# A three-part decoder layer on one core: the first feed-forward group's routing laid between the pieces of the last cross-attention step

## The chip, the cores and the metric

The kernel runs on one core of a Trainium2 chip. The metric is the device time of one execution in microseconds. The median of three runs before the change is 622.98 us (621.36 to 623.25). The engines are TensorE (PE, with its weight loads as PEld), VectorE (DVE), ScalarE (ACT), GpSimd (POOL) and SyncE (SP). Each runs its own queue strictly in the order written, and they meet at semaphores.

## What is computed

The input is a stream x of 32 batches of 128 x 128 floats. Three blocks follow each other, each a layer norm, a block and a residual addition.

```python
x = x + gated_slot_attention(layernorm(x))                    # recurrent, 4 heads
x = x + cross_attention(layernorm(x), ctx, bias, mask)        # 16 heads of 8, full softmax
x = x + experts(layernorm(x))
# experts: logits = h @ gate_w.T + gate_b; scores = softmax(logits); top-2 of 8
# for e in range(8):
#   gate  = (times e is among the two) * (sum of the two scores)
#   inter = h @ wi.T + bi + (h @ lora_A[e].T) @ lora_B[e].T
#   out  += gate * (relu(inter) @ wo.T + bo)
```

## The kernel before

The kernel has three stages, one per block. Each is a software pipeline: a step function per engine (x_tensor, x_scalar, x_vector and x_pool for cross attention; f_tensor, f_scalar, f_vector and f_pool for the feed-forward) holds that engine's share of one step, with flags that say which phases a step has. Steady steps stand in a loop; the first and the last are written out ("peeled") by x_peeled and f_peeled, which work out the flags. The order of the work is the order of these calls in each engine's block, written out by hand; there is no planner.

**Cross attention.** A step n handles one batch in each phase: it normalises batch n+3, projects batch n+2, makes the scores of batch n+1, turns the attention weights of batch n ("attend"), and finishes batch n-1. Step 30 has scores of batch 31, attends to batch 30 and finishes batch 29. Step 31 attends to batch 31 and finishes batch 30, and has no scores left. Step 32 only finishes batch 31. In a step ScalarE takes 16 exponentials of 128 x 128 in four groups of four (L960), TensorE transposes each group (L916), VectorE or ScalarE copies it out of PSUM (L1056 on VectorE, L986 on ScalarE), TensorE mixes the values (L927), VectorE multiplies by the reciprocals (L1051), TensorE applies the output weight (L903), and VectorE adds the result to the stream X (L1070). VectorE also makes the reciprocals (L1060) and spreads them (L1065); TensorE turns these (L888) and ScalarE copies them (L981).

**Feed-forward.** A tick f(t) handles groups of four batches: it normalises group t+1, routes group t and runs the experts of group t-1. Tick f(-1) only normalises group 0, and tick f(0) normalises group 1 and routes group 0 without expert work. f(1) is the first full tick, f(1) to f(6) have the same load, and f(7) is the last that routes and normalises nothing. The route on the engines:

- TensorE: x_turned (L1210, four transposes), logits (L1217), lora_inner (L1223), choices_turned (L1230, eight transposes).
- ScalarE: the copy of the transposes (L1298), gate_exps (L1316), the lora copies (L1308, L1311), x_high (L1303).
- VectorE: statistics (L1351, L1355), logits (L1368 to L1371), ranks (L1376 to L1386), choices (L1394, L1395), gates (L1399 to L1407), chosen_inner (L1415), normalise (L1362).
- POOL: x_low (L1471), roots (L1464, L1467), u_low (L1475), output_bias (L1481, L1484).

The expert work on TensorE is L1236 and L1260, with L1293 on ScalarE and L1422 and L1431 on VectorE.

**Where the two stages meet.** Every engine's block ends its cross stage in the same order: the tick f(-1), then steps 30 and 31, then f(0), then step 32, then f(1) and the loop. TensorE waits before f(0) until all scores have been taken out of their PSUM banks (the tick writes the same banks), and before f(1) until every batch has its cross output:

```python
x_peeled(cross, 30); x_peeled(cross, 31)
pe.wait_ge(C["tt"], 4 * B)
f_peeled(experts, 0)
x_peeled(cross, B)
pe.wait_ge(C["x2"], B)
f_peeled(experts, 1)
```

(B is 32; the first line is a loop in the source.)

Of the kernel before, what the change touches and what calls it, by code (L numbers as in the profile page):

```python
# [15 lines left out]
B, T, D = 32, 128, 128  # L16
# [8 lines left out]
GROUPS = B // GROUP  # L25
# [25 lines left out]
def decoder(nc, x, ctx_in, fside, amask, kmask, g_wq, g_wk, g_wv, g_wf, g_norm, g_wo,  # L51
# [6 lines left out]
    with stack:  # L58
# [801 lines left out]

        SCORE_BANKS = (1, 4, 5, 6)

        def x_tensor(pe, m, q, norm, project, scores, attend, finish):
            n = 2 * m + q
            o = 1 - q

            def all_scores():

                need(pe, C["q"], n + 2)
                need(pe, C["kbd"], n + 2)  # L870
                need(pe, C["tt"], 4 * n + 4)
                for i in range(NI):
                    rows = slice(32 * i, 32 * i + 32)
                    nc.tensor.matmul(bank(SCORE_BANKS[i]), qx[rows, o, :], kbd[rows, o, :, :].rearrange("p j s -> p (j s)"),  # L874
                                     start=True, stop=True).then_inc(C["sc"], 1)

            def inputs_turned():
                need(pe, C["xn"], n + 3)
                need(pe, s_ctx[q], 16 * (m + 2))
                need(pe, C["x2"], n - 1)  # L880
                need(pe, C["v"], n + 1)
                nc.tensor.transpose(bank(0)[:, 0:128], xn2[:], ident[:])
                nc.tensor.transpose(bank(0)[:, 128:256], ctxb[:, q, :], ident[:]).then_inc(C["Tp"], 1)
# [45 lines left out]
                                                PTs[:, o, i, 128 * j:128 * j + 128], start=(j == 0), stop=(j == XG - 1))  # L929
                last.then_inc(C["pv"], 1)  # L930

            if scores:
                all_scores()
            if project:
                inputs_turned()
            if finish:
                reciprocals_turned()
            if attend:
                weights_turned(0)
                weights_turned(1)  # L940
            if project:
                queries_keys()
            if finish:
                mix_values()
            if attend:
                weights_turned(2)
            if scores or finish:
                outputs_values()
            if attend:
                weights_turned(3)  # L950

        def x_scalar(act, m, q, norm, project, scores, attend, finish):
            n = 2 * m + q
            o = 1 - q

            def exps(batch, par, i):

                need(act, C["tt"], 4 * batch + i + 1)
                for h in range(XG * i, XG * i + XG):
                    last = nc.scalar.activation(P[:, par, h, :], P[:, par, h, :], ACT.Exp, bias=mn[:, par, h:h + 1], scale=-1.0,  # L960
                                                accum_out=rsx[:, par, h:h + 1])
                last.then_inc(C["ex"], 1)

            def inputs_turned():
# [12 lines left out]

            def reciprocals_turned():
                need(act, C["Rp"], n)
                need(act, C["oT"], n - 1)  # L980
                nc.scalar.copy(RT[:], bank(7)[:, 0:128]).then_inc(C["RT"], 1)  # L981

            def weights_turned():
                need(act, C["pt"], 4 * n + 4)
                need(act, C["pv"], n - 1)
                nc.scalar.copy(PTs[:, q, 3, :], bank(3)).then_inc(C["ptA"], 1)  # L986

            if attend:
                exps(n, q, 1)
            if project:  # L990
                inputs_turned()
            if finish:
                reciprocals_turned()
            if attend:
                exps(n, q, 2)
            if project:
                queries_keys()
            if attend:
                exps(n, q, 3)
            if scores:  # L1000
                exps(n + 1, o, 0)
            if attend:
                weights_turned()

        def x_row(m, q, k):

            n = 2 * m + q + k
            return X[:, n, :] if isinstance(n, int) else X[:, bass.ds(n, 1), :].rearrange("p a d -> p (a d)")

        def x_vector(dve, m, q, norm, project, scores, attend, finish):  # L1010
            n = 2 * m + q
            o = 1 - q

# [64 lines left out]
            if project:  # L1078
                masks()
            if norm:  # L1080
                statistics()
                aggregates()
            if scores:
                score(0)
            if attend:
                weights_turned(0)
            if scores:
                score(1)
            if attend:
                weights_turned(1)  # L1090
            if scores:
                score(2)
            if finish:
                outputs()
            if scores:
                score(3)
            if attend:
                weights_turned(2)
            if scores:
                values()  # L1100
            if finish:
                add_to_stream()
            if attend:
                reciprocals()
                reciprocals_spread()
            if norm:
                normalise()

        def x_pool(pool, m, q, norm, project, scores, attend, finish):
            n = 2 * m + q  # L1110

            def output_bias():
# [28 lines left out]
                roots()  # L1141

        def x_peeled(step, n):
            step(n // 2, n % 2, *(0 <= n + k < B for k in (3, 2, 1, 0, -1)))

        def x_loop(engine, step):
            with engine.Fori(1, B // 2 - 2, 1) as m:
# [52 lines left out]
        s_out = [sem(f"stored{i}") for i in range(2)]  # L1201

        def f_tensor(pe, m, q, norm, route, expert):
            t = 2 * m + q
            def x_turned():
                need(pe, M["xn"], t + 1)
# [53 lines left out]
                                                woT[:, c, :], start=(c == 0), stop=(c == FC - 1))  # L1261
                last.then_inc(M["y"], 1)

            if route:
                x_turned()
            if expert:
                first(0)
            if route:
                logits()
            if expert:  # L1270
                second(0)
                first(1)
            if route:
                lora_inner()
            if expert:
                second(1)
# [1 line left out]
                first(3)  # L1278
                second(2)
                second(3)  # L1280
            if route:
                choices_turned()
            if expert:
                down()

        def f_scalar(act, m, q, norm, route, expert):
            t = 2 * m + q
            p = t - 1

# [28 lines left out]
            if route:  # L1318
                x_turned()
            if expert:  # L1320
                relu(0)
            if route:
                gate_exps()
            if expert:
                relu(1)
            if route:
# [6 lines left out]
        def f_vector(dve, m, q, norm, route, expert):  # L1333
            t = 2 * m + q
            p, o = t - 1, 1 - q

# [98 lines left out]
            if norm:  # L1435
                statistics()
            if route:
                logits()
            if expert:
                hidden(0)  # L1440
            if route:
                ranks()
            if expert:
                hidden(1)
            if route:
                choices()
                gates()
            if expert:
                hidden(2)
                hidden(3)  # L1450
            if route:
                chosen_inner()
            if norm:
                normalise()
            if expert:
                add_to_stream()

        def f_pool(pool, m, q, norm, route, expert):
            t = 2 * m + q

            def roots():
# [24 lines left out]
            if route:  # L1486
                x_low()
            if norm:
                roots()
            if route:  # L1490
                u_low()
                output_bias()

        def f_peeled(tick, t):
            tick(t // 2, t % 2, *(0 <= t + k < GROUPS for k in (1, 0, -1)))

        def f_loop(engine, tick):
            with engine.Fori(1, GROUPS // 2 - 1, 1) as m:
# [26 lines left out]
        def _(pool):  # L1526
# [28 lines left out]
                x_peeled(cross, n)  # L1555
            pool.wait_ge(C["xn"], B)
            f_peeled(experts, -1)
            for n in range(B - 2, B):
                x_peeled(cross, n)
            f_peeled(experts, 0)  # L1560
            x_peeled(cross, B)
            f_peeled(experts, 1)
            f_loop(pool, experts)
# [4 lines left out]
        def _(act):  # L1568
# [27 lines left out]
            act.wait_ge(s_small, SMALL)  # L1596
            act.wait_ge(G["x1"], PAIRS)
            f_peeled(experts, -1)
            for n in range(B - 2, B):
                x_peeled(cross, n)  # L1600
            f_peeled(experts, 0)
            x_peeled(cross, B)
            f_peeled(experts, 1)
            f_loop(act, experts)
# [4 lines left out]
        def _(dve):  # L1609
# [43 lines left out]
            for n in range(B - 2, B):  # L1653
                x_peeled(cross, n)
            f_peeled(experts, 0)
            x_peeled(cross, B)
            dve.wait_ge(C["x2"], B)
            f_peeled(experts, 1)
# [5 lines left out]
        def _(pe):  # L1664
# [37 lines left out]
            for n in range(B - 2, B):  # L1702
                x_peeled(cross, n)
            pe.wait_ge(C["tt"], 4 * B)
            f_peeled(experts, 0)
            x_peeled(cross, B)
            pe.wait_ge(C["x2"], B)
            f_peeled(experts, 1)
# [27 lines left out]
```

## Time and profile before

| | |
|---|---|
| median of three runs | 622.98 us (621.36 to 623.25) |
| the profiled execution's own time | 620.23 us |
| its span, from first to last instruction | 618.5 us |
| mean granted TensorE clock | 0.96 |
| busy: TensorE / VectorE / ScalarE / POOL | 511.4 / 497.3 / 432.0 / 369.5 us |

The rows are from one execution. Times count from the start of the span. "Idle before" in brackets is the time for which the engine had nothing to run ahead of the row, and names what ended it.
### The profile page before, as it was taken

Reading aid. Unit: us, or ns where it says so; the run is one execution under the profiler, and the core shown is the slowest. Engines: PE = TensorE matmul, PEld = TensorE weight load, DVE = VectorE, ACT = ScalarE, POOL = GpSimd, SP = SyncE. Lnnn points to the kernel's source line nnn. Section 1 sums busy time; section 2 is a strip of 40 time slices with the busy share of each in tenths; the row PEclk is TensorE's granted clock in tenths of the full one; section 3 lists DMA queues with packets and bytes.
Section 4 is the critical chain, followed back from the end, with each engine's and each line's share of the span. In section 5 each row is a group of like instructions: output and inputs, shape, how many; then the busy total and the mean of one; then the engine's idle time right before and its main releaser. Section 6 shows DMA issues by size and latency. Waiting matters only on the chain. (4 is left out here: it accounts for less than half of the span.)

```text
span 618.5 us, 15993 instructions
## 1 busy us (share of the span) xinstructions
PE 511.4 (83%) x4272; PEld 380.2 (61%) x4272; DVE 497.3 (80%) x2009; ACT 432.0 (70%) x1545; POOL 369.5 (60%) x392
## 2 busy tenths in 40 slices
PE   4689999999996768777777777777766899999986
PEld 3466777777774445555555555555545678788874
DVE  2677888888876269999999999999986788898872
ACT  2668787887872269999999999999984333333321
POOL 6236554555534778888888888888932233444430
PEclk9899999999998669999999999999997799999999
DMA  6910000000000447888888888888700000000000
GB/s 159 239 21 1 1 2 0 0 0 0 2 1 2 72 98 130 144 144 146 144 145 143 149 146 145 147 147 147 119 2 2 0 18 19 17 17 17 19 18 17
DMA packets 84422, 42.37 MB, mean 69 GB/s; under 512 B 4378, under 2 KB 84132, under 8 KB 84388
## 3 DMA queue, kind: packets, MB, share of 16 engines
q1 hardware_dynamic: 83234, 41.63, 36.6%
q10 hardware_dynamic: 1154, 0.33, 0.2%
q8 instruction: 16, 0.26, 0.2%
q14 instruction: 18, 0.15, 0.1%
HBM read 39.86 MB, written 2.10 MB: 68 GB/s over the span
## 5 line engine op out<-in xcount | busy, mean ns | idle before, releaser
L960 ACT ACTIVATE c_P<-c_P,c_min 128x128 f32<-128x128 f32 x512 | 204.7, 461 | 0.0
L1129 POOL TENSOR_TENSOR c_bias<-c_fside,c_cm 128x2048 f32<-128x2048 f32 x32 | 145.4, 4545 | 2.7 <-DVE c_cm L1046 2.7
L960 ACT ACTIVATION_READ_ACCUMULATOR c_P<-c_P,c_min 128x1 f32 x512 | 132.8, 260 | 0.0
L1021 DVE CUSTOM_DVE_ANT_0 c_P<-banks,c_bias 128x128 f32<-128x128 f32 x512 | 117.0, 285 | 7.9 <-issue 3.6
L916 PE MATMUL banks<-ident,c_P 128*128 128x128 f32 x512 | 80.7, 286 | 8.1 <-ACT c_P L960 6.4
L916 PEld LDWEIGHTS banks<-ident,c_P 128*128 128x128 f32 x512 | 57.5, 144 | 22.6 <-ACT c_P L960 12.9
L1056 DVE COPY shared<-banks 128x512 f32<-128x512 f32 x96 | 65.9, 686 | 2.8 <-PE banks L916 2.8
L1471 POOL TENSOR_TENSOR xs<-shared,xs 128x512 fp32r<-128x512 f32 x8 | 10.7, 1343 | 85.7 <-ACT xs L1303 85.7
L1236 PE MATMUL banks<-um,lb_s 128*128 128x512 f32 x192 | 55.7, 405 | 2.7 <-ACT shared L1293 1.9
L1293 ACT ACTIVATE shared<-banks,bi_col 128x512 f32<-128x512 f32 x32 | 22.0, 688 | 38.9 <-PE banks L1236 38.9
L903 PE MATMUL banks<-x_wT,shared 128*128 128x128 f32 x64 | 15.2, 321 | 40.1 <-DVE shared L1051 40.1
L1236 PEld LDWEIGHTS banks<-um,lb_s 128*128 128x128 f32 x192 | 34.4, 189 | 18.9 <-ACT shared L1293 12.4
L793 POOL TENSOR_TENSOR shared<-shared 128x512 f32<-128x512 f32 x16 | 20.4, 1275 | 38.4 <-ACT shared L584 38.4
L1021 DVE DVE_READ_ACCUMULATOR2_ANT c_min<- 128x1 f32 x512 | 42.5, 83 | 0.0
L874 PE MATMUL banks<-shared,c_q 32*128 32x512 f32 x256 | 38.4, 670 | 2.4 <-DVE X L726 0.5
L903 PEld LDWEIGHTS banks<-x_wT,shared 128*128 128x128 f32 x64 | 10.0, 197 | 46.8 <-issue 43.5
L452 PEld LDWEIGHTS banks<-shared 128*128 128x128 f32 x256 | 29.8, 192 | 13.0 <-DVE shared L679 13.0
L927 PE MATMUL banks<-shared,c_vpad 128*32 128x128 f32 x1024 | 36.3, 285 | 0.6 <-ACT shared L981 0.6
L1298 ACT COPY shared<-banks 128x512 f32<-128x512 f32 x8 | 4.7, 588 | 43.4 <-PE banks L1210 43.4
L1134 POOL TENSOR_TENSOR shared<-c_k,k_mask 128x512 f32<-128x512 f32 x32 | 33.3, 1042 | 0.4 <-ACT c_k L976 0.4
L452 PE MATMUL banks<-shared 128*128 128x64 f32 x256 | 32.0, 278 | 1.9 <-DVE shared L679 1.9
L1260 PE MATMUL banks<-woT,shared 128*128 128x128 f32 x256 | 30.7, 279 | 2.1 <-DVE shared L1422 1.9
(197 smaller groups left out, 1340.9 us busy)
## 6 DMA issues: line engine op xcount, KB each, us to landing
c_fside<-in_fside_Bx16xSxS_dram SPq DMA_DIRECT2D x64, 512.0 KB, 7.2
c_ctx<-in_ctx_dram SPq DMA_DIRECT2D x32, 64.0 KB, 5.3
out_dram<-shared SPq DMA_DIRECT2D x8, 256.0 KB, 2.3
X<-in_x_dram SPq DMA_DIRECT2D x3, 512.0 KB, 5.4
kmask_sb<-in_mask_BxS_bf_dram SPq DMA_DIRECT2D x1, 512.0 KB, 7.2
X<-in_x_dram SPq DMA_DIRECT2D x2, 128.0 KB, 3.5
c_P<-in_L_ffn_wi_dram SPq DMA_DIRECT2D x1, 256.0 KB
c_P<-in_L_ffn_lora_B_dram SPq DMA_DIRECT2D x1, 256.0 KB
```

What stands on the lines that cost most here:

```text
L452: last = nc.tensor.matmul(bank(4)[:, 256 * b + GM * h:256 * b + GM * h + GM], Am[:, 4 * (h // 2) + 2 * b + h % 2, :], sp_[:, q, b, GM * h: ...
L874: nc.tensor.matmul(bank(SCORE_BANKS[i]), qx[rows, o, :], kbd[rows, o, :, :].rearrange("p j s -> p (j s)"), start=True, stop=True).then_inc ...
L903: last = nc.tensor.matmul(bank(0)[:, 0:128], oTs[:], x_wT[:, 3, :], start=True, stop=True)
L916: last = nc.tensor.transpose(bank(2 + i % 2)[:, 128 * j:128 * j + 128], P[:, q, XG * i + j, :], ident[:])
L927: last = nc.tensor.matmul(bank(7)[32 * i:32 * i + 32, 0:128], vp[:, o, VPAD * i + 32 * j:VPAD * i + 32 * j + 32], PTs[:, o, i, 128 * j:128 ...
L960: last = nc.scalar.activation(P[:, par, h, :], P[:, par, h, :], ACT.Exp, bias=mn[:, par, h:h + 1], scale=-1.0, accum_out=rsx[:, par, h:h + 1])
L1021: last = nc.vector.tensor_tensor_reduce(out=P[:, o, h, :], in0=bank(SCORE_BANKS[i])[:, 128 * j:128 * j + 128], in1=fm[:, o, h, :], scale=- ...
L1056: nc.vector.tensor_copy(PTs[:, q, i, :], bank(2 + i % 2)).then_inc(C["ptD"], 1)
L1129: nc.gpsimd.tensor_tensor(fm[:, q, :, :], fs[:, q, :, :], bc(cm[:], XH), ALU.add).then_inc(C["fm"], 1)
L1134: nc.gpsimd.tensor_tensor(kbd[:, q, :, :], bc(kx[:], XG), inner(k_mask[:], 128), ALU.mult).then_inc(C["kbd"], 1)
L1236: last = nc.tensor.matmul(out, weight[:, a, :], moving[:, b, :], start=start and k == 0, stop=stop and k == len(PASSES) - 1, **also)
L1260: last = nc.tensor.matmul(bank(7)[:, 128 * b:128 * b + 128], hT[:, c, 128 * b:128 * b + 128], woT[:, c, :], start=(c == 0), stop=(c == FC ...
```

## The change

Steps and ticks take a list of parts, so that one can be issued in pieces. For a cross step there are two parts. Part 0 ends on TensorE after the first group's transposes, on ScalarE after the second group's exponentials and the two copies, and on VectorE after the copy of the first group. For a tick there are four:

- part 0: the transposes of the normalised group (TensorE, ScalarE), the statistics of the next group (VectorE), its roots (POOL)
- part 1: logits and lora_inner (TensorE), gate_exps, lora copies and x_high (ScalarE), logits, ranks and choices (VectorE), x_low (POOL)
- part 2: choices_turned (TensorE), gates and chosen_inner (VectorE), u_low and output_bias (POOL)
- part 3: normalise (VectorE)

On each engine f(0) is then laid around and inside step 31. VectorE takes part 3 before part 2. On POOL, which has no work in steps 30 to 32, only roots and x_low change places. TensorE's wait for the scores moves ahead of part 0. Instructions and semaphore counts are the same.

```diff
@@ VectorE's block (POOL and ScalarE end with f_peeled(experts, 0, (2, 3)))
-            for n in range(B - 2, B):
-                x_peeled(cross, n)
-            f_peeled(experts, 0)
+            x_peeled(cross, B - 2)
+            f_peeled(experts, 0, (0,))
+            x_peeled(cross, B - 1, (0,))
+            f_peeled(experts, 0, (1,))
+            x_peeled(cross, B - 1, (1,))
+            f_peeled(experts, 0, (3,))
+            f_peeled(experts, 0, (2,))
             x_peeled(cross, B)
@@ TensorE's block
-            for n in range(B - 2, B):
-                x_peeled(cross, n)
+            x_peeled(cross, B - 2)
             pe.wait_ge(C["tt"], 4 * B)
-            f_peeled(experts, 0)
+            f_peeled(experts, 0, (0,))
+            x_peeled(cross, B - 1, (0,))
+            f_peeled(experts, 0, (1,))
+            x_peeled(cross, B - 1, (1,))
+            f_peeled(experts, 0, (2,))
             x_peeled(cross, B)
@@ f_vector (the other step functions likewise)
-            if route:
+            if route and 1 in parts:
                 choices()
+            if route and 2 in parts:
                 gates()
```

## Rows read from the trace of the kernel before

**Rows 1.** Windows: length; PE, PEld, DVE, ACT, POOL busy (instructions); clock; DMA share, GB/s.
```profile
440.00:460.00 20.00, 15.00 (x179) 10.38 (x179) 18.07 (x115) 20.00 (x103) 13.77 (x10) 1.00 0.29 50
463.80:470.00 6.20, 6.16 (x51) 5.10 (x52) 2.60 (x6) 4.40 (x24) 0.00 (x0) 0.50 0.01 3
470.00:477.00 7.00, 2.71 (x16) 1.64 (x14) 5.29 (x21) 3.02 (x6) 1.62 (x3) 0.99 0.00 0
477.00:484.80 7.80, 4.90 (x44) 3.82 (x44) 6.59 (x18) 0.27 (x1) 4.99 (x4) 0.50 0.00 1
484.80:487.00 2.20, 2.20 (x8) 1.91 (x9) 1.21 (x8) 0.59 (x1) 0.00 (x0) 0.50 0.00 0
502.00:582.00 80.00, 79.05 (x451) 64.09 (x451) 71.49 (x205) 26.47 (x45) 32.78 (x30) 1.00 0.05 17
```

**Rows 2.** Timeline of VectorE in the transition: start, us, line, operation [idle before].
```profile
463.56 0.23 DVE L1065 COPY shared<-shared 128x128 f32<-128x128 f32 x1
465.20 0.69 DVE L1056 COPY shared<-banks 128x512 f32<-128x512 f32 x1 [1.42 <-PE banks L916]
...
470.30 0.87 DVE L1351 BATCH_NORM_STATS2 stats<-X 128x6 f32<-128x128 f32 x4
471.30 0.38 DVE L1355 BATCH_NORM_AGGREGATE meanvar<-stats 128x2 f32<-128x6 f32 x4
472.51 0.19 DVE L1368 TENSOR_TENSOR shared<-banks,gb_sb 128x32 f32<-128x32 f32 x1 [0.83 <-PE banks L1217]
...
473.52 0.18 DVE L1376 TENSOR_SCALAR shared<-shared 128x32 f32<-128x32 f32 x1 [0.37 <-ACT shared L1316]
...
475.97 0.87 DVE L1394 TENSOR_SCALAR shared<-shared 128x512 f32<-128x512 f32 x1
476.88 0.69 DVE L1395 SCALAR_TENSOR_TENSOR shared<-shared 128x512 f32<-128x512 f32 x1
...
478.45 1.24 DVE L1407 TENSOR_TENSOR shared<-shared 128x4 f32<-128x4 f32 x1
479.78 2.48 DVE L1415 TENSOR_TENSOR um<-banks,shared 128x512 fp32r<-128x512 f32 x4
482.18 1.10 DVE L1362 TENSOR_SCALAR shared<-X,meanvar,rstd 128x128 f32<-128x128 f32 x4
```

**Rows 3.** Timeline of TensorE in the transition and at the first ticks.
```profile
463.84 0.47 PE L888 MATMUL banks<-ident,shared 128*128 128x128 f32 x1 [1.04 <-DVE shared L1065]
464.11 2.02 PE L916 MATMUL banks<-ident,c_P 128*128 128x128 f32 x8
...
471.41 1.06 PE L1217 MATMUL banks<-gwT,shared 128*128 128x8 f32 x8 [0.73 <-ACT shared L1298]
472.33 1.10 PE L1223 MATMUL banks<-shared,laT 128*128 128x512 f32 x2
477.62 1.97 PE L1230 MATMUL banks<-ident,shared 128*128 128x128 f32 x8 [4.19 <-DVE shared L1395]
...
484.78 1.11 PE L1210 MATMUL banks<-ident,shared 128*128 128x128 f32 x4 [0.39 <-DVE X L1070]
...
497.07 1.03 PE L1230 MATMUL banks<-ident,shared 128*128 128x128 f32 x8
...
501.81 0.66 PE L1210 MATMUL banks<-ident,shared 128*128 128x128 f32 x4
```

**Rows 4.** Timeline of ScalarE in the transition.
```profile
463.31 0.41 ACT L960 ACTIVATE c_P<-c_P,c_min 128x128 f32<-128x128 f32 x1
...
473.47 0.58 ACT L1308 COPY shared<-banks 128x512 f32<-128x512 f32 x1
...
474.61 0.61 ACT L1303 CAST xs<-shared 128x512 fp32r<-128x512 f32 x1
```

**Rows 5.** VectorE in the last routing tick, f(7).
```profile
589.98 1.67 DVE L1395 SCALAR_TENSOR_TENSOR shared<-shared 128x512 f32<-128x512 f32 x1
591.57 1.26 DVE L1399 TENSOR_SCALAR shared<-shared 128x32 f32<-128x32 f32 x1
```

More of the change, by code:

```diff
@@ L861, in decoder, with x_tensor @@
         SCORE_BANKS = (1, 4, 5, 6)
-        def x_tensor(pe, m, q, norm, project, scores, attend, finish):
+        def x_tensor(pe, m, q, norm, project, scores, attend, finish, parts=(0, 1)):
             n = 2 * m + q
@@ L930, in mix_values, with x_scalar @@
                 last.then_inc(C["pv"], 1)
[L932 to L952, printed above, removed]
+            if 0 in parts:
+                if scores:
+                    all_scores()
+                if project:
+                    inputs_turned()
+                if finish:
+                    reciprocals_turned()
+                if attend:
+                    weights_turned(0)
+            if 1 in parts:
+                if attend:
+                    weights_turned(1)
+                if project:
+                    queries_keys()
+                if finish:
+                    mix_values()
+                if attend:
+                    weights_turned(2)
+                if scores or finish:
+                    outputs_values()
+                if attend:
+                    weights_turned(3)
+        def x_scalar(act, m, q, norm, project, scores, attend, finish, parts=(0, 1)):
             n = 2 * m + q
@@ L986, in weights_turned @@
                 nc.scalar.copy(PTs[:, q, 3, :], bank(3)).then_inc(C["ptA"], 1)
[L988 to L1003, printed above, removed]
+            if 0 in parts:
+                if attend:
+                    exps(n, q, 1)
+                if project:
+                    inputs_turned()
+                if finish:
+                    reciprocals_turned()
+            if 1 in parts:
+                if attend:
+                    exps(n, q, 2)
+                if project:
+                    queries_keys()
+                if attend:
+                    exps(n, q, 3)
+                if scores:
+                    exps(n + 1, o, 0)
+                if attend:
+                    weights_turned()
         def x_row(m, q, k):
@@ L1008, in x_row, with x_vector @@
             return X[:, n, :] if isinstance(n, int) else X[:, bass.ds(n, 1), :].rearrange("p a d -> p (a d)")
-        def x_vector(dve, m, q, norm, project, scores, attend, finish):
+        def x_vector(dve, m, q, norm, project, scores, attend, finish, parts=(0, 1)):
             n = 2 * m + q
@@ L1076, in values, with x_pool @@
                 nc.vector.tensor_copy(dst, bank(0)[:, 128:256].rearrange("p (i j d) -> p i j d", i=NI, j=XG)).then_inc(C["v"], 1)
[L1078 to L1109, printed above, removed]
+            if 0 in parts:
+                if project:
+                    masks()
+                if norm:
+                    statistics()
+                    aggregates()
+                if scores:
+                    score(0)
+                if attend:
+                    weights_turned(0)
+            if 1 in parts:
+                if scores:
+                    score(1)
+                if attend:
+                    weights_turned(1)
+                if scores:
+                    score(2)
+                if finish:
+                    outputs()
+                if scores:
+                    score(3)
+                if attend:
+                    weights_turned(2)
+                if scores:
+                    values()
+                if finish:
+                    add_to_stream()
+                if attend:
+                    reciprocals()
+                    reciprocals_spread()
+                if norm:
+                    normalise()
+        def x_pool(pool, m, q, norm, project, scores, attend, finish, parts=(0, 1)):
             n = 2 * m + q
@@ L1141, in x_pool, with x_peeled @@
                 roots()
-        def x_peeled(step, n):
-            step(n // 2, n % 2, *(0 <= n + k < B for k in (3, 2, 1, 0, -1)))
+        def x_peeled(step, n, parts=(0, 1)):
+            step(n // 2, n % 2, *(0 <= n + k < B for k in (3, 2, 1, 0, -1)), parts)
         def x_loop(engine, step):
@@ L1201, in decoder, with f_tensor @@
         s_out = [sem(f"stored{i}") for i in range(2)]
-        def f_tensor(pe, m, q, norm, route, expert):
+        def f_tensor(pe, m, q, norm, route, expert, parts=(0, 1, 2, 3)):
             t = 2 * m + q
@@ L1262, in down @@
                 last.then_inc(M["y"], 1)
-            if route:
+            if route and 0 in parts:
                 x_turned()
@@ L1267, in f_tensor @@
                 first(0)
-            if route:
+            if route and 1 in parts:
                 logits()
@@ L1272, in f_tensor @@
                 first(1)
-            if route:
+            if route and 1 in parts:
                 lora_inner()
@@ L1280, in f_tensor @@
                 second(3)
-            if route:
+            if route and 2 in parts:
                 choices_turned()
@@ L1284, in f_tensor, with f_scalar @@
                 down()
-        def f_scalar(act, m, q, norm, route, expert):
+        def f_scalar(act, m, q, norm, route, expert, parts=(0, 1, 2, 3)):
             t = 2 * m + q
@@ L1316, in gate_exps @@
                 nc.scalar.activation(ex[:], lgt[:], ACT.Exp).then_inc(M["ex"], 1)
-            if route:
+            if route and 0 in parts:
                 x_turned()
@@ L1321, in f_scalar @@
                 relu(0)
-            if route:
+            if route and 1 in parts:
                 gate_exps()
@@ L1325, in f_scalar @@
                 relu(1)
-            if route:
+            if route and 1 in parts:
                 lora_inner()
@@ L1331, in f_scalar, with f_vector @@
                 relu(3)
-        def f_vector(dve, m, q, norm, route, expert):
+        def f_vector(dve, m, q, norm, route, expert, parts=(0, 1, 2, 3)):
             t = 2 * m + q
@@ L1433, in add_to_stream @@
                 last.then_inc(M["out"], 1)
-            if norm:
+            if norm and 0 in parts:
                 statistics()
-            if route:
+            if route and 1 in parts:
                 logits()
@@ L1440, in f_vector @@
                 hidden(0)
-            if route:
+            if route and 1 in parts:
                 ranks()
@@ L1444, in f_vector @@
                 hidden(1)
-            if route:
+            if route and 1 in parts:
                 choices()
+            if route and 2 in parts:
                 gates()
@@ L1450, in f_vector @@
                 hidden(3)
-            if route:
+            if route and 2 in parts:
                 chosen_inner()
-            if norm:
+            if norm and 3 in parts:
                 normalise()
@@ L1456, in f_vector, with f_pool @@
                 add_to_stream()
-        def f_pool(pool, m, q, norm, route, expert):
+        def f_pool(pool, m, q, norm, route, expert, parts=(0, 1, 2, 3)):
             t = 2 * m + q
@@ L1484, in output_bias, with f_peeled @@
                 nc.gpsimd.tensor_tensor(x3, x3, gated_bias[:], ALU.add).then_inc(M["added"], 1)
-            if route:
+            if route and 1 in parts:
                 x_low()
-            if norm:
+            if norm and 0 in parts:
                 roots()
-            if route:
+            if route and 2 in parts:
                 u_low()
                 output_bias()
-        def f_peeled(tick, t):
-            tick(t // 2, t % 2, *(0 <= t + k < GROUPS for k in (1, 0, -1)))
+        def f_peeled(tick, t, parts=(0, 1, 2, 3)):
+            tick(t // 2, t % 2, *(0 <= t + k < GROUPS for k in (1, 0, -1)), parts)
         def f_loop(engine, tick):
@@ L1557, in _ @@
             f_peeled(experts, -1)
-            for n in range(B - 2, B):
-                x_peeled(cross, n)
-            f_peeled(experts, 0)
+            x_peeled(cross, B - 2)
[3 more added lines that the diff above has]
+            x_peeled(cross, B - 1, (1,))
+            f_peeled(experts, 0, (2, 3))
             x_peeled(cross, B)
@@ L1598, in _ @@
             f_peeled(experts, -1)
-            for n in range(B - 2, B):
-                x_peeled(cross, n)
-            f_peeled(experts, 0)
+            x_peeled(cross, B - 2)
[3 more added lines that the diff above has]
+            x_peeled(cross, B - 1, (1,))
+            f_peeled(experts, 0, (2, 3))
             x_peeled(cross, B)
@@ L1652, in _ @@
             f_peeled(experts, -1)
-            for n in range(B - 2, B):
-                x_peeled(cross, n)
-            f_peeled(experts, 0)
+            x_peeled(cross, B - 2)
+            f_peeled(experts, 0, (0,))
+            x_peeled(cross, B - 1, (0,))
+            f_peeled(experts, 0, (1,))
+            x_peeled(cross, B - 1, (1,))
+            f_peeled(experts, 0, (3,))
+            f_peeled(experts, 0, (2,))
             x_peeled(cross, B)
@@ L1701, in _ @@
             f_peeled(experts, -1)
-            for n in range(B - 2, B):
-                x_peeled(cross, n)
+            x_peeled(cross, B - 2)
             pe.wait_ge(C["tt"], 4 * B)
-            f_peeled(experts, 0)
+            f_peeled(experts, 0, (0,))
+            x_peeled(cross, B - 1, (0,))
+            f_peeled(experts, 0, (1,))
+            x_peeled(cross, B - 1, (1,))
+            f_peeled(experts, 0, (2,))
             x_peeled(cross, B)
```

## The prediction

> **What bounds the kernel now.** I read the busy time by stage first. The cross stage is set by ScalarE, busy 20.00 of 20 us, and the feed-forward by TensorE, busy 79.05 of 80 us [rows 1]. Between them, from 463.8 to 484.8 us, no engine is full. VectorE is the busiest with 2.60 + 5.29 + 6.59 = 14.5 of 21.0 us, and TensorE's granted clock is 0.50, the 1.2 GHz level, in two of the three stretches. The timelines by engine say why. VectorE finishes step 30 at 463.79 (L1065) and then waits for step 31's pieces (1.42 us before L1056) [rows 2], while TensorE, ScalarE and VectorE hand each other small things. Only then comes the first group's route, alone: gate logits L1217 at 471.41, VectorE's chain from L1368 at 472.51 to the choices' end at 477.57 (476.88 + 0.69), for which TensorE idles 4.19 us (L1230), then gates, chosen rows, normalise [rows 2, 3]. Last, TensorE waits for the last stream addition and starts the first full tick f(1) at 484.78; the next starts at 501.81 [rows 3]. As TensorE is full from there on, a microsecond by which f(1) starts sooner is a microsecond off the end.
>
> **The change part by part.** No instruction is added or dropped and no DMA is issued or moved: SP's only later duty, the stores, waits for f(1)'s result as before. Up to 463.79 all engines run as now, but for one piece. So the sum is the time of f(1)'s start, worked out from there, with TensorE low to 470 as now.
>
> *The transposes moved ahead (f(0) part 0).* TensorE's wait for all scores comes forward; the whole TensorE queue stands behind it. TensorE idles 1.04 us before 463.84 anyway (L888, which waits for VectorE's L1065) [rows 3], and step 31's scores are VectorE work older than L1065. Four transposes are half of L1230's eight, 0.5 us at the full clock and 1.0 at the low one (1.03 and 1.97 for eight) [rows 3]. Taken as nothing; without that gap 1.0. ScalarE's copy of them (like L1308, 0.58) delays its four exponentials by 0.6, which nothing waits for yet [rows 4].
>
> *Statistics, then the first weights.* Statistics run 470.30 to 471.68, 1.38 us [rows 2]: now 463.79 to 465.2, in the stretch where VectorE sat idle. TensorE finishes the first four of L916's eight transposes at about 465.1 (half of 2.02 after 464.11) [rows 3]; VectorE copies them, 0.69 (L1056), to 465.9. POOL's roots follow the statistics and are early.
>
> *Gate, ranks, choices (part 1).* Logits: 1.06 at the full clock [rows 3]; at the low one about 2.0 (estimate, by the 1.97/1.03 of L1230), so 465.1 to 467.1. From L1368 to the choices' end is 5.06 us now [rows 2]; put at 467.2 it ends at 472.25. VectorE waits at its head for the logits (1.3 us) and then 0.4 for ScalarE's exponential, with the second weights' copy and everything of step 31 queued behind. ScalarE waits in its turn for the shifted logits; behind it stand the lora copies and eight exponentials of step 31, and for those TensorE's weights 2 and 3 and VectorE's reciprocals. The lora product (1.10, low 2.1) ends at 469.2; the three copies take 473.47 to 475.22 = 1.75 [rows 3, 4], so 471.0; eight exponentials at 0.39 (0.41 the row, overlapping) end at 474.1.
>
> *The rest of step 31 on VectorE.* Weights 1, output product, weights 2, stream addition: 0.69 + 0.28 + 0.69 + 0.28 = 1.94 (the 128x128 pieces as long as the rows' 0.23 to 0.34) [rows 2], to 474.2. That is the same moment as ScalarE's last exponential: from here on a delay of either counts fully. Reciprocals and spread 0.4: 474.6.
>
> *Normalise, gates, chosen rows.* Normalise 1.10 [rows 2]: 475.7. Gates took 477.57 to 479.69 with L1407 at 1.24, against 0.18 for a wider instruction (L1376): it stood behind POOL. POOL's u_low is now long done, so the gates cost 2.12 - 1.06 = 1.06: 476.8. Chosen rows 2.48: 479.3; their eight transposes and step 32's mix lie beside this on TensorE. The tail from the end of normalise (483.28) to f(1) (484.78) is 1.50 [rows 2, 3]: f(1) starts at 480.8. **Saving: 484.78 - 480.8 = 4.0 us.** It is VectorE's idle 6.5 us and L1407's 1.06, less what stays idle: the new 1.3 and 0.4, 0.9 in the tail, and 1.0 of pieces that I added end to end and that overlap a little.
>
> *Where it can be off.* With TensorE at the full clock throughout, the logits are there when the first copy ends: choices end at 470.95, ScalarE is no longer beside the path, f(1) at 479.5, saving 5.3; f(1) also ran its first 2.2 us at 0.50 [rows 1], which would give back 1.1 more: 6.4. On the other side stands POOL. x_low and u_low now follow each other without the roots between, right behind x_high, at about 471.0, beside the choices' second instruction. The last tick, where they also follow each other, shows L1395 at 1.67 against 0.69 and L1399 at 1.26 against 0.18 [rows 2, 5], about 1.0 each. I take none of them, since the 5.06 contains L1394 at its 0.87 beside x_low; one would make the saving 3.0, two 2.0.
>
> The Trainium skill, "SBUF — State Buffer", section "Who interferes with whom", says that a VectorE instruction with two SBUF inputs, or in a two-port mode, shares a port pair with GpSimd and that the second to start is blocked for the whole instruction of the first. By it I would charge one block, as L1395 and x_low come at the same time, and f(1) would start at 481.8; the rows of the last tick agree in size.
>
> Against the profiled execution (620.23 us, of which 618.5 span) 4.0 us gives 616.2. The runs' median is 2.75 above that execution; shifted by it, **619.0 us**.
>
> **The rivals.** *Full clock.* The 0.5 us of transposes before 463.3 keep the clock up. For it: that work is new in a gap. Against: the transition stays thin. Saving 6.4: 616.6.
>
> *The clock stays low in f(1).* TensorE's work is now spread over the whole transition with waits between. In rows 1 the clock was 0.50 through 6.2 us of nearly full work (6.16 busy) before it rose, against 2.2 us in f(1) now. If f(1) needs 6.2, it loses (6.2 - 2.2)/2 = 2.0: saving 2.0, 621.0. Against: TensorE is busier in 474 to 480 than it was.
>
> The Trainium skill, "TensorE: Matmul & The Clock Gate", Part 1, says the default is the throttled state and activity releases it, which speaks for this rival. By it f(1) could open low whatever the transition saves. The clock's fall at 477 behind 7.0 us in which TensorE was busy 2.71 [rows 1] agrees.
>
> *ScalarE becomes the bound.* Its copies and eight exponentials run behind the choices, not beside them: 472.25 + 1.75 + 3.1 = 477.1, TensorE's last transposes 1.0, reciprocals at 478.1 instead of 474.2. That eats 3.9 of the 4.0: 622.9. For it: the two shares end together in my sum. Against: they can only slip so far if the lora product ends after 472. The same time follows if something else than the stream addition holds f(1), against which L1210's idle time names it.
>
> *The clock stays low through the first full tick.* This is the slower side: place f(1) to 497, price half a microsecond for each. It decides once the low stretch lasts over (4.0 + 1.9 + 1.1) x 2 = 14 us of f(1); for all of it (17.0 long, 15.9 of full-clock work) the loss is 14.8 - 4.0: 633.8. Against: no dense stretch of the trace stayed low over 6.2 us.
>
> **How the numbers follow.** Forecast (saving 3.0 to 5.4, 617.6 to 620.0): 0.61. Full clock: 0.07. Low clock in f(1): 0.13, of which 0.09 is still clearly faster. ScalarE bound or f(1) held otherwise: 0.12. Low for a tick: 0.07. A measurement of this kernel tells about 0.3%, 1.9 us, from no change. Faster 0.61 + 0.07 + 0.09 = 0.77, same 0.04 + 0.12 = 0.16, slower 0.07. The range 616.6 to 621.6 takes in full clock, both POOL blocks, and the low clock in f(1).
>
> **What would show it.** Right: L1210's first transposes at about 462.8, before L888; L1368 near 467 and the choices' end near 472 to 473; L1407 at about 0.2; f(1)'s x2 wait ending near 481 and the next tick 16 to 17 us later. Wrong: ScalarE's last exponential after 476, L1395 or its neighbour over 1.6 twice, a granted clock of 0.50 beyond 484, or f(1) released by anything but L1070.

## The result and the profile after

The changed kernel runs in 615.5 us (613.52 to 616.14), the kernel before in 623.12 us beside it: ratio 0.9878, 95% interval 0.9851 to 0.9906, that is 7.6 us or 5.8 to 9.3. The forecast was the right sign and too small: 619.0 us, range 616.6 to 621.6.

To see where the time went I cut each profile at three events that every kernel here has: (c) is the time from the start to the end of VectorE's spread copy of step 30 (up to there VectorE's order is the same), (a) from there to f(1)'s first transposes, (b) from those to the next tick's. The rest of the span is 116.6 to 116.8 us in every profile, and an execution's own time is 1.7 to 1.8 us longer than its span.

| kernel, profile | (c) | (a) | (b) | that execution |
|---|---|---|---|---|
| before, the first profile | 463.79 | 20.99 | 17.03 | 620.23 |
| before, again (e7a) | 463.96 | 21.69 | 19.93 | 624.07 |
| before, again (e7b) | 463.97 | 22.18 | 17.21 | 621.79 |
| changed | 462.61 | 16.66 | 15.92 | 613.52 |
| changed, again (e1) | 464.99 | 16.67 | 15.97 | 616.07 |

Between the first profiles, 6.7 us apart, (a) gives 4.3, (b) 1.1 and (c) 1.2. The last is not the change's: (c) was 465.0 in the changed kernel's next profile.

VectorE in the changed kernel, as in [rows 2] (L1070 is before's L1065, L1061 is L1056, L1375 to L1402 are L1368 to L1395, L1414 and L1422 are L1407 and L1415):
```profile
462.38 0.23 DVE L1070 COPY shared<-shared 128x128 f32<-128x128 f32 x1
462.52 0.87 DVE L1358 BATCH_NORM_STATS2 stats<-X 128x6 f32<-128x128 f32 x4
463.52 0.38 DVE L1362 BATCH_NORM_AGGREGATE meanvar<-stats 128x2 f32<-128x6 f32 x4
464.16 0.69 DVE L1061 COPY shared<-banks 128x512 f32<-128x512 f32 x1 [0.26 <-PE banks L916]
465.14 0.19 DVE L1375 TENSOR_TENSOR shared<-banks,gb_sb 128x32 f32<-128x32 f32 x1 [0.29 <-PE banks L1224]
...
468.60 0.88 DVE L1401 TENSOR_SCALAR shared<-shared 128x512 f32<-128x512 f32 x1
469.51 1.64 DVE L1402 SCALAR_TENSOR_TENSOR shared<-shared 128x512 f32<-128x512 f32 x1
...
472.90 0.29 DVE L1075 TENSOR_TENSOR X<-banks,X 128x128 f32<-128x128 f32 x1 [0.35 <-PE banks L903]
...
473.53 1.11 DVE L1369 TENSOR_SCALAR shared<-X,meanvar,rstd 128x128 f32<-128x128 f32 x4
...
475.52 0.16 DVE L1414 TENSOR_TENSOR shared<-shared 128x4 f32<-128x4 f32 x1
475.60 2.48 DVE L1422 TENSOR_TENSOR um<-banks,shared 128x512 fp32r<-128x512 f32 x4
```
The waits of [rows 2] (1.42, 0.83) have shrunk to 0.26 and 0.29. L1402 has grown to 1.64. POOL's two subtractions, x_low (L1479) and u_low (L1483), now follow each other: L1401 stands beside the first, with 0.88 much as before (0.87), and L1402 starts behind the second, which it did not meet before:
```profile
467.93 1.26 POOL L1479 TENSOR_TENSOR xs<-shared,xs 128x512 fp32r<-128x512 f32 x1 [2.66 <-ACT xs L1310]
469.15 1.45 POOL L1483 TENSOR_TENSOR shared<-shared 128x512 fp32r<-128x512 f32 x1
```
TensorE in the changed kernel, as in [rows 3] (L1217 is the group's transposes, L1224 the logits):
```profile
462.31 1.06 PE L1217 MATMUL banks<-ident,shared 128*128 128x128 f32 x4
463.16 0.42 PE L888 MATMUL banks<-ident,shared 128*128 128x128 f32 x1
...
464.04 1.06 PE L1224 MATMUL banks<-gwT,shared 128*128 128x8 f32 x8
...
469.46 0.66 PE L916 MATMUL banks<-ident,c_P 128*128 128x128 f32 x4 [1.95 <-ACT c_P L963]
472.10 0.77 PE L903 MATMUL banks<-x_wT,shared 128*128 128x128 f32 x2 [1.98 <-DVE shared L1056]
...
479.27 0.66 PE L1217 MATMUL banks<-ident,shared 128*128 128x128 f32 x4 [0.39 <-DVE X L1075]
...
495.19 0.66 PE L1217 MATMUL banks<-ident,shared 128*128 128x128 f32 x4
```
And its windows, columns as in [rows 1]:
```profile
470.60:477.40 6.80, 4.75 (x40) 4.41 (x44) 6.28 (x20) 1.19 (x4) 1.57 (x3) 0.51 0.01 4
477.40:479.20 1.80, 0.85 (x18) 0.42 (x9) 1.16 (x4) 0.00 (x0) 0.75 (x1) 1.00 0.00 0
479.20:495.20 16.00, 15.84 (x91) 12.86 (x91) 13.21 (x38) 5.30 (x9) 6.55 (x6) 1.00 0.00 1
```
The transition still has 6.8 us at 1.2 GHz, but they are over before f(1), which runs at 2.4 GHz throughout. Before, f(1) opened low [rows 1].

### The profile page after: what moved, and what is told of

Same layout as the page of the kernel before. It is cut to its first block and busy times, and to the rows that moved or that the text cites. A ratio compares the mean times of both kernels' runs of the same rounds, so it can differ in the third digit from the quotient of the medians.

```text
span 611.8 us, 15993 instructions
## 1 busy us (share of the span) xinstructions
PE 509.7 (83%) x4272; PEld 378.8 (62%) x4272; DVE 497.3 (81%) x2009; ACT 431.5 (71%) x1545; POOL 369.2 (60%) x392
## 5 line engine op out<-in xcount | busy, mean ns | idle before, releaser
L963 ACT ACTIVATE c_P<-c_P,c_min 128x128 f32<-128x128 f32 x512 | 215.9, 577 | 0.0
L963 ACT ACTIVATION_READ_ACCUMULATOR c_P<-c_P,c_min 128x1 f32 x512 | 173.7, 376 | 0.0
L916 PE MATMUL banks<-ident,c_P 128*128 128x128 f32 x512 | 83.0, 286 | 22.9 <-ACT c_P L963 20.3
L1061 DVE COPY shared<-banks 128x512 f32<-128x512 f32 x96 | 65.8, 686 | 0.7 <-PE banks L916 0.7
L1479 POOL TENSOR_TENSOR xs<-shared,xs 128x512 fp32r<-128x512 f32 x8 | 10.7, 1338 | 66.8 <-ACT xs L1310 66.8
L1243 PEld LDWEIGHTS banks<-um,lb_s 128*128 128x128 f32 x192 | 34.2, 188 | 18.9 <-ACT shared L1300 12.5
L1429 DVE SCALAR_TENSOR_TENSOR shared<-banks,neg_bi,shared 128x512 f32<-128x512 f32 x32 | 23.5, 750 | 11.1 <-PE banks L1243 10.7
```

Source lines behind the costliest of these rows:

```text
L916: last = nc.tensor.transpose(bank(2 + i % 2)[:, 128 * j:128 * j + 128], P[:, q, XG * i + j, :], ident[:])
L1061: nc.vector.tensor_copy(PTs[:, q, i, :], bank(2 + i % 2)).then_inc(C["ptD"], 1)
L1243: last = nc.tensor.matmul(out, weight[:, a, :], moving[:, b, :], start=start and k == 0, stop=stop and k == len(PASSES) - 1, **also)
```

## The experiments

**e1, e7a, e7b: both kernels profiled again.**

> The changed kernel unaltered, a second profile and five timed rounds. Three spans are compared with the profiles so far: (a) end of VectorE's spread copy of step 30 to f(1)'s first transposes, 20.99 us before and 16.66 after; (b) f(1) to the second full tick, 17.03 before and 15.92 after; (c) start to that spread copy, 463.79 before and 462.61 after. Theory A (the handovers): the gain is (a), which repeats at 16.7 +- 0.5. Theory B (the clock's luck): a good part of the 7.6 us lies in (b) and (c), where TensorE's clock happened to be up, and a second look shows (b) nearer 17.0, (c) nearer 463.8, and a median ratio nearer 0.991. If A holds with the clock as part of the change, (b) stays near 15.9 and the ratio near 0.988.

Measured: 615.59 us, ratio 0.9867 (0.984 to 0.9894); (a) 16.67, (b) 15.97, (c) 464.99. Span (a) and f(1)'s clock repeat; (c) does not.

> The kernel before, unaltered, another look. Spans: (c) start to the end of step 30's spread copy, (a) from there to f(1)'s transposes, (b) f(1) to the next tick. Theory A (handovers, with the gain in (a) alone): (a) 21.0, (b) 17.0, (c) 463.8 as in the first profile. Theory B (the first profile is a lucky one, as its 620.2 us lies below the median 622.8): (a) again 20.5 to 21.5, but (b) or (c) 1 to 3 us longer, with the granted clock 0.50 for longer after f(1) starts, or earlier in the transition between the first two stages.

> The kernel before, unaltered, a third look, as the one ahead of it. Theory A: (a) 21.0, (b) 17.0, (c) 463.8. Theory B: (a) 20.5 to 21.5, (b) 17 to 19 and (c) 463 to 466, each with the stretches of low clock that explain it.

Measured: the first row of the table was the cheapest of three. The window after f(1)'s start in e7a, columns as in [rows 1]:
```profile
485.60:494.90 9.30, 9.25 (x28) 7.76 (x29) 4.18 (x17) 1.56 (x4) 0.00 (x0) 0.52 0.00 0
494.90:505.60 10.70, 10.60 (x64) 8.40 (x62) 8.98 (x21) 3.73 (x6) 6.58 (x6) 1.00 0.01 2
```
f(1) ran its first 8.9 us at the low clock, and in the 9.30 us of the first window TensorE was busy for 9.25; (b) was 19.93. Over the three profiles (a) + (b) is 38.0, 41.6 and 39.4, mean 39.7; over the two of the changed kernel 32.6. The difference, 7.1 us, is the measured gain within its interval. That the kernel before spends more time at the low clock is no accident of the profiles: its mean granted clock over a whole execution is 0.950 to 0.964 in the 54 executions timed beside the experiments, the changed kernel's 0.963 to 0.978 in ten.

**e2: part 0 alone ahead of step 31.** On every engine (TensorE shown):
```diff
-            f_peeled(experts, 0, (1,))
             x_peeled(cross, B - 1, (1,))
+            f_peeled(experts, 0, (1,))
             f_peeled(experts, 0, (2,))
```

> One part alone: only part 0 (transposes of the group, their copy, the statistics and roots of the next group) is laid ahead of step 31; gate, ranks, choices, gates and normalise follow it as before. Theory A: the idle time before step 31's pieces takes 1.4 us of statistics off VectorE's chain and about 1.2 us of ScalarE's and TensorE's copy and transposes: saving 1.5 to 2.5 us, so 620.5 to 621.5. Theory C (the whole gain sits in part 0, because TensorE's clock is kept up by the early transposes): about 616. Theory D (the gain comes only from ranks and choices beside step 31): about 623.

Measured: 622.18 us, ratio 0.9972 (0.9948 to 0.9995); (a) 20.46, (b) 18.95. Part 0 takes no more than 1.7 us off (a) against the three profiles of the kernel before (20.99 to 22.18), and f(1) runs partly low (granted clock 0.82 over its 18.9 us). Part 0 neither holds the gain nor keeps the clock. But VectorE's order differs in one more thing: normalise (part 3) stands behind the gates and chosen rows (part 2) again, as in the kernel before, and there the chosen rows wait for the choices' transposes at the low clock:
```profile
476.57 1.63 DVE L1402 SCALAR_TENSOR_TENSOR shared<-shared 128x512 f32<-128x512 f32 x1
...
480.26 2.48 DVE L1422 TENSOR_TENSOR um<-banks,shared 128x512 fp32r<-128x512 f32 x4 [1.02 <-PE banks L1237]
```
Of the 3.8 us by which (a) is longer than in the changed kernel, up to 1.0 can be this order; no run has it alone. At least 2.8 go with the gate, ranks and choices beside step 31.

**e4, e10: the kernel before with TensorE kept busy.** In f(0), ahead of the choices' transposes (e4), and besides ahead of step 32's output product (e10); the conditions that keep the loops to this tick and step, and a wait ahead of the second, are left out here:
```diff
+            for k in range(28):
+                nc.tensor.transpose(bank(5 + k % 2)[:, 0:128], ident[:], ident[:])
             choices_turned()
@@ e10 also, in step 32
+            for k in range(20):
+                nc.tensor.transpose(bank(1)[:, 0:128], ident[:], ident[:])
             outputs_values()
```

> The kernel before, with 28 transposes of the identity (some 3.6 us at the full clock) put on TensorE into the 4.2 us in which it waits for the choices; their output is overwritten. Theory A with the clock as a term of its own: the clock does not fall to 1.2 GHz ahead of f(1), so f(1) takes 16.0 instead of 17.0 us and the tail ahead of it 0.3 to 0.5 less: 621.4 to 621.9. Rival (the clock falls for another reason, or the fall in this stretch is chance): 623.1, with f(1) at 17.0.

Measured: 622.26 us, ratio 0.9983 (0.9967 to 1.0); (a) 21.51, (b) 17.56. The clock fell again, now at 483.2, in the 3.50 us gap ahead of step 32's output product, and the first 3.5 us of f(1) were low.

> The kernel before with the 28 filler transposes in the wait for the choices and 20 more (2.5 us at the full clock) ahead of step 32's output product, where TensorE idled 3.5 us once the first fillers kept its clock up; outputs overwritten. With the first fillers alone the clock still fell ahead of f(1), and (b), f(1) to the next tick, was 17.56. Theory B' (part of the gain is a low clock that the kernel before carries into f(1): (b) was 17.0, 19.9 and 17.2 in three looks, and 15.9 and 16.0 in two of the changed kernel): (b) falls to 16.0, (a) stays at 21 to 22, and the median is 1 to 2.5 us below the kernel before, 620.2 to 621.7. Rival (the low clock in f(1) comes from something else than the thin stretch ahead of it): no change, (b) 17 to 20.

Measured: 620.35 us, ratio 0.9953 (0.9934 to 0.9971), 2.9 us; (a) 20.70, (b) 15.94. Its windows of the transition and of f(1), columns as in [rows 1]:
```profile
470.00:484.40 14.40, 10.80 (x107) 8.99 (x105) 11.82 (x37) 3.30 (x7) 6.62 (x6) 1.00 0.01 2
484.40:500.40 16.00, 15.85 (x91) 12.86 (x91) 13.19 (x37) 5.30 (x9) 6.55 (x6) 1.00 0.00 1
```
With nothing laid elsewhere, holding the clock through the thin stretch is worth 2.9 us to the kernel before. Between this kernel and the changed one, both with f(1) at full clock, (a) differs by 20.70 - 16.66 = 4.04 us. That is nearly the handovers alone, but not quite: the clock came back 6.2 us after the spread copy here and 1.1 us after it there. Against e5 (below), where it came back after 5.5 us, the difference is 20.70 - 17.09 = 3.61 us. The runs' medians differ by more, 620.35 against 615.5.

**e5: the changed kernel with fillers in its two gaps.** In step 31 alone (the condition is left out here):
```diff
+                    keep_busy(12)      # 12 transposes of the identity
                     weights_turned(2)
+                    keep_busy(12)
                     outputs_values()
```

> The changed kernel with twelve transposes of the identity (1.5 us at the full clock) ahead of the third weights' transposes of step 31 and twelve ahead of its output product, where TensorE waits 1.95 and 1.98 us; their output is overwritten. Theory A with the clock as a term: the clock does not fall in 470 to 478, the eight transposes of the choices and step 32's mix run at full speed, which lie beside VectorE: 0.2 to 0.6 us of gain, 615.0 to 615.4. Theory B (clock luck decides): the times draw together, highest to lowest below 1.5 us, with the same median. Rival: the fillers themselves delay the transposes where the clock is already low, 616 to 617.

Measured: 618.24 us, ratio 0.9937 (0.9913 to 0.9961), 2.7 us above the changed kernel's median, and the intervals of the two ratios do not meet. Windows, columns as in [rows 1]; f(1) starts at 483.13:
```profile
472.00:482.00 10.00, 6.85 (x104) 5.97 (x92) 9.00 (x24) 4.58 (x20) 5.29 (x4) 0.99 0.01 2
483.10:493.00 9.90, 9.87 (x29) 7.77 (x29) 4.69 (x18) 2.19 (x4) 0.00 (x0) 0.55 0.00 0
```
(a) moved little, 17.09, but (b) was 19.90: the clock fell at 481.8, just ahead of f(1), in a gap that had no fillers (2.50 us ahead of step 32's output product), and f(1)'s first 8.9 us are low. None of the three expectations had that.

**e3, e11: x_low behind the choices.** M["hot"] is the semaphore of the choices:
```diff
                 need(pool, M["x_high"], t + 1)
+                if isinstance(t, int) and t == 0:
+                    need(pool, M["hot"], 1)
```

> The changed kernel with one wait more on POOL: in f(0) x_low waits for the choices, so that neither x_low nor u_low runs beside the choices. In the changed kernel's profile these took 0.88 and 1.64 us instead of 0.42 and 0.69. Theory A (VectorE's chain is what f(1) waits for): the choices end 1.4 us sooner and f(1) starts 0.8 to 1.4 us sooner, 614.1 to 614.7. Rival (TensorE and ScalarE are next, as the output product and the last exponentials end within 0.4 us of VectorE's share): no more than 0.4 us.

> x_low behind the choices alone, another look and more times. Theory B': (a) is again 14.8 +- 0.3, and the times fall into two groups some 3 to 4 us apart by whether (b) is 16.0 or 19 to 20; a slow look shows (b) at 19 or more. Rival (the spread comes from the start of the cross stage, (c)): (b) 16.0 in every look and (c) up to 468.

Measured: 616.17 us, 0.989 (0.9858 to 0.9923), and 616.97 us, 0.9896 (0.986 to 0.9932): no better than the change. Yet (a) is 14.77 and 15.47, and VectorE's two choices in e3 are:
```profile
470.44 0.43 DVE L1401 TENSOR_SCALAR shared<-shared 128x512 f32<-128x512 f32 x1
470.90 0.69 DVE L1402 SCALAR_TENSOR_TENSOR shared<-shared 128x512 f32<-128x512 f32 x1
```
So POOL did cost 0.45 + 0.95 us. Without it f(1) starts 1.2 us sooner in e11; the 1.9 of e3 are not POOL's alone, as the clock there did not fall in the transition before 471.3 and the logits reached VectorE 0.75 us sooner. In e11 (b) is 17.34, with the clock at 0.91 over f(1): it fell at 473.4, was up at 476.8, and fell again at 480.2, 0.4 us ahead of f(1). The times reach from 613.35 to 619.3, and the clock goes with them: the four executions up to 614.92 had a mean granted clock of 0.971 to 0.974, the eight from 615.7 up 0.963 to 0.969. That (b) accounts for all of the spread is likely, not shown: two profiles don't place every time.

**e6, e9, e8: x_low late, with fillers in the middle (as in e5), ahead of step 32's output product, and in both.** Conditions and a wait are left out again:
```diff
@@ e9 and e8, in step 32 (12 and 16 fillers)
+                for k in range(12):
+                    nc.tensor.transpose(bank(1)[:, 0:128], ident[:], ident[:])
                 outputs_values()
```

> The changed kernel with both: x_low behind the choices, and the filler transposes. With x_low late alone, f(1) started 14.8 us after step 30's spread copy instead of 16.7 in the profiles, but the median did not move and the times spread from 614.4 to 619.3. Theory B (TensorE, thinly used, drops to the low clock in f(1) in some executions and loses up to 3 us there): with the filler the low executions go and the median is 613.5 to 614.5. Rival (x_low late costs elsewhere, such as the first expert product that needs it): the median stays at 615.5 to 616.5.

> The changed kernel with x_low behind the choices, and 12 filler transposes only ahead of step 32's output product, where TensorE idled 2.0 us in that version; outputs overwritten. Theory B' : x_low late shortens (a) to 14.8, but leaves that gap right ahead of f(1), and where the clock falls there f(1) runs low (its times spread from 614.4 to 619.3). Filling the gap keeps (b) at 16.0: median 613.5 to 614.5, spread below 3 us. Rival (fillers move the fall into f(1), as those in the middle did): (b) near 19.5, 617 to 618.

> x_low behind the choices, fillers in the two gaps in the middle and 16 more ahead of step 32's output product. Fillers in the middle alone cost 2 us: (b) was 19.6 and 19.9, with the clock falling 1 to 2 us ahead of f(1) instead of 9. Theory B': with the last gap filled too there is no fall at all, (a) 14.8 to 15.2, (b) 16.0: 613.3 to 614.3. Rival (the fillers cost by themselves, by holding TensorE's queue): 616 to 618 again, with (b) at 16 and (a) at 17.

| | us | ratio | (a) | (b) |
|---|---|---|---|---|
| e6, fillers in the middle | 617.7 (616.2 to 621.69) | 0.9929 (0.9907 to 0.995) | 15.09 | 19.60 |
| e9, fillers at the end | 614.06 (613.42 to 616.08) | 0.986 (0.9829 to 0.9891) | 15.43 | 15.95 |
| e8, both | 614.11 (613.99 to 615.02) | 0.986 (0.9831 to 0.9889) | 14.77 | 15.97 |

e6 is low in f(1), as e5 was. With the last gap filled (b) is 16.0, whether the middle is filled (e8: granted clock 1.00 all through) or not (e9: the low stretch ends at 479.0, ahead of f(1) at 481.17). For e9 the profile proves little, as e3 had 15.94 without any filler. No cost of the fillers shows: e8 has the most, and its (a) is e3's 14.77. e8 and e9 have lower medians than the changed kernel, by about 1.5 us, but their intervals overlap its own; that they beat it is likely, not settled.

## Why the prediction was wrong

Point by point, in microseconds after step 30's spread copy, from the first profile of the changed kernel:

| step | predicted | measured |
|---|---|---|
| logits reach VectorE | 3.4 | 2.5 |
| choices end | 8.5 | 8.5 |
| normalise starts | 10.8 | 10.9 |
| chosen rows end | 15.5 | 15.5 |
| f(1) starts | 17.0 | 16.7 |

- *The handovers were right.* Predicted saving in (a) 4.0; measured 4.3 between the first profiles, and 4.04 or 3.6 against e10. L1414 fell to 0.16 as said, and f(1) was released by the stream addition (L1075).
- *Two errors inside cancelled, so that the points agree to 0.3 us is in part luck.* The clock rose at 463.7, 1.1 us after the copy, and not at 470, so logits took 1.06 and not 2.0; and POOL, which I charged nothing, took 0.95 of L1402. That is one block beyond the one that the 5.06 contained: u_low had started 0.36 us ahead of L1402, and e3 shows both instructions short again with POOL out of the way. One block is what the Trainium skill's rule ("SBUF — State Buffer", "Who interferes with whom") had charged. Whether the early transposes brought the clock back is not shown: e4, without them, also had it back after 1.1 us, and e5, with them, after 5.5; there (a) was 17.09.
- *The transposes ahead did not fit their gap for nothing*, as they ran at the low clock: L1217 1.06, up to 463.16 against a spread copy ending at 462.61. TensorE came 0.5 late to the reciprocals, and VectorE's statistics covered it. ScalarE was not beside the path: its last exponential ended at 470.85, 8.2 after the copy and not 10.3.
- *The step that failed is the last of the sum*: "The runs' median is 2.75 above that execution; shifted by it, 619.0 us". I took the 2.75 for a constant, and f(1)'s 2.2 us at the low clock [rows 1] for what both kernels pay: in "a microsecond by which f(1) starts sooner is a microsecond off the end" f(1) is as long after the change as before, a term put at nothing. Two more profiles show 17.2 and 19.9 for (b), mean of three 18.1, while the changed kernel had 15.9 and 16.0. The three profiled executions average 622.0, so 1.8 of the 2.75 was the first one's luck, and 1.7 of that lies in (a) and (b). The gain has a second term, about 2.1 in (b), that the prediction held only as a rival of 0.07, and sized 1.1 there from one profile. e10 isolates it: 2.9 us (1.8 to 4.1) with the order of before; in its profile 2.1 in (b) and 0.9 in (a) against the means of the three. With the 3.6 to 4.0 of the handovers that makes 6.5 to 6.9, inside the measured interval.
- *The low-clock rival had the right mechanism on the wrong kernel.* I feared that the change would carry a low clock into f(1). It is the kernel before that does. The ground against a longer low stretch, that no dense stretch stayed low over 6.2 us, did not hold either: in e7a f(1) was low for 8.9, and the first profile itself has the clock low for 17.1 us from 210.6, with TensorE busy for 12.58 of them. The Trainium skill's sentence that the default is the throttled state ("TensorE: Matmul & The Clock Gate", Part 1) agrees with both kernels, but does not say which of them is low at f(1).

The clock falls ahead of f(1) in both kernels. The last fall in the transition, in microseconds, by the granted clock of each profile:

| profile | fall, ahead of f(1) | clock low for | of that in f(1) | (b) |
|---|---|---|---|---|
| before, the first | 7.9 | 10.2 | 2.3 | 17.03 |
| before, e7a | 8.2 | 17.1 | 8.9 | 19.93 |
| before, e7b | 11.0 | 13.7 | 2.8 | 17.21 |
| e4 | 3.3 | 6.8 | 3.5 | 17.56 |
| e10 | none | 0 | 0 | 15.94 |
| changed | 8.8 | 6.8 | 0 | 15.92 |
| changed, e1 | 8.7 | 6.8 | 0 | 15.97 |
| e2 | 0.9 behind its start | 6.8 | 6.8 | 18.95 |
| e5 | 1.3 | 10.2 | 8.9 | 19.90 |

Span (b) goes with the part of f(1) that is low. It does not go with where the fall lies: that is 8 to 11 us ahead of f(1) in the three profiles of the kernel before and nearly 9 us ahead in the changed one. What differs is how long the clock then stays low. In the changed kernel TensorE was busy for 4.65 and 4.77 of the 6.8 us until the clock was back; in the kernel before for 4.9 of the 7.9, 8.2 and 11.0 us up to f(1), and it was still low.

Open is what brings the clock back: why after 6.8 us in the changed kernel, and why after 2.3 us of f(1) in one execution of the kernel before and after 8.9 in another. The runs show only that it does.

## What to carry to other kernels

Lay a dense stage's first small chain between the pieces of the stage ahead and count the idle time of the engine that carries both: that sum held to 0.3 us here, with two errors that cancelled. Ask besides at which clock the dense stage opens, in more than one profile, as a low opening cost up to 4 us here. If its clock is to be held by filler work, fill the last gap too: fillers in earlier gaps alone left f(1) low (e4, e5, e6), fillers in those and the last did not (e8, e10). When the profiled execution lies well below the median, look for what the others pay before you treat the difference as a constant.

## What the runs showed of the hardware that I had not expected

TensorE stayed at 1.2 GHz through the first 8.9 us of f(1) in e7a and in e5, where [rows 1] had 2.2; its windows there show it busy for 9.25 of 9.30 us and for 9.87 of 9.90; in e2 the clock fell 0.9 us after f(1) had begun. Transposes of the identity whose output nobody reads, put into both gaps of the kernel before, were worth 2.9 us (e10), and 1.1 (0 to 2.1) in the first gap alone (e4); put into the changed kernel's two gaps 7 to 10 us ahead of f(1), with the last left open, they cost 2.7 (e5).
